# A token-sorted mixture of low-rank experts on one core: tiles of one expert instead of two, its projections made beforehand

## The reference

```python
conf = sigmoid(einsum('bsh,eh->bse', x, conf_W) + conf_b)
top_bids, sel = top_k(conf * expert_wealth, 2)
routing = softmax(top_bids)
for e in range(8):
    g = x @ base_gate + x @ gate_A[e] @ gate_B[e] * 0.25
    u = x @ base_up   + x @ up_A[e]   @ up_B[e]   * 0.25
    h = silu(g) * u
    oe = h @ base_down + h @ down_A[e] @ down_B[e] * 0.25
    out += sum(routing * (sel == e), -1)[..., None] * oe
return x + tanh(g_ffn) * out
```

## Time and profile before

| | |
|---|---|
| median of 3 runs | 350.17 us (349.76 to 350.34) |
| profiled execution: span from first to last instruction | 343.0 us |
| TensorE busy | 262.8 us, 77% |
| VectorE busy | 220.6 us, 64% |
| ScalarE busy | 160.7 us, 47% |
| GpSimd busy | 129.1 us, 38% |
| moved by DMA | 45.67 MB, 133 GB/s |

### The profile page before, as it was taken

How to read it: one execution, slowest core, us unless ns; L and a number is a source line. 1 busy time by engine, 2 the same in 40 slices (tenths; PEclk the granted TensorE clock), 3 DMA queues, 4 the chain that set the end, 5 groups by cost and what they waited for, 6 DMA issues and landing times.

```text
span 343.0 us, 5103 instructions
## 1 busy us (share of the span) xinstructions
PE 262.8 (77%) x1500; PEld 229.4 (67%) x1501; DVE 220.6 (64%) x433; ACT 160.7 (47%) x277; POOL 129.1 (38%) x148
## 2 busy tenths in 40 slices
PE   3474363537278899995999999999999999998600
PEld 2251241214167799994999999999999999997500
DVE  2979975798952881006666777777777777775325
ACT  0443875196336363343455555555555555555211
POOL 3528376537441441109233333333333333311121
PEclk9996566555579899998999999999999999999965
DMA  7803333013663646446244444434344444420065
GB/s 259 240 23 80 70 84 84 26 51 107 177 158 134 210 167 267 175 164 214 44 139 139 139 138 133 143 135 141 134 138 142 138 136 138 140 106 15 15 193 190
DMA packets 30189, 45.67 MB, mean 133 GB/s; under 512 B 13976, under 2 KB 25632, under 8 KB 30176
## 3 DMA queue, kind: packets, MB, share of 16 engines
q0 software_dynamic: 4416, 21.50, 18.9%
q1 hardware_dynamic: 20752, 14.03, 14.6%
q10 hardware_dynamic: 5008, 9.98, 7.9%
HBM read 33.57 MB, written 11.93 MB: 133 GB/s over the span
## 4 chain that ended last, share of the span: by engine, by line
PE 65%; DVE 17%; issue 5%; DMA 4%; POOL 3%; ACT 3%; SPq 1%; DVEq 0%; ACTq 0%; POOLq 0%
PE pY L55 8%; PE pY L59 7%; PE pY L57 7%; PE pG L55 5%; PE pT L1395 5%; PE pG L59 4%; PE pG L57 4%; PE pU L57 4%; PE pU L55 4%; PE pU L59 4%; DMA x_resid<-in_x_dram 2%; DVE q L899 2%; DMA yr<-results 1%; DVE q L819 1%; DVE am L821 1%
## 5 line engine op out<-in xcount | busy, mean ns | idle before, releaser
L496 POOL DMA_INDIRECT results<-yb,dest x19 | 19.0, 998 | 91.9 <-DVE yb L1108 91.9
L55 PE MATMUL pY<-Wd_hi,hT_hi 128*128 128x384 f32 x133 | 47.5, 357 | 0.9 <-ACT Wd_lo L694 0.8
L59 PE MATMUL pY<-Wd_hi,hT_lo 128*128 128x384 f32 x133 | 44.7, 336 | 0.0
L57 PE MATMUL pY<-Wd_lo,hT_hi 128*128 128x384 f32 x133 | 44.6, 336 | 0.0
L490 POOL DMA_INDIRECT bin<-base_products,tok x18 | 22.0, 1221 | 24.8 <-PE pU L59 15.2
L704 ACT CAST hT_hi<-pT 128x896 fp32r<-128x896 f32 x19 | 17.2, 907 | 24.1 <-PE pT L1395 24.1
L680 ACT CAST xaT_hi<-pX 128x256 fp32r<-128x256 f32 x19 | 7.1, 373 | 42.5 <-PE pX L1372 42.0
L55 PEld LDWEIGHTS pY<-Wd_hi,hT_hi 128*128 128x128 f32 x133 | 25.0, 188 | 2.3 <-DVE hT_lo L1096 1.0
L57 PEld LDWEIGHTS pY<-Wd_lo,hT_hi 128*128 128x128 f32 x133 | 25.1, 188 | 0.0
L482 POOL DMA_INDIRECT xin<-normed,tok x19 | 18.6, 979 | 16.9 <-PE pX L1358 9.9
L59 PEld LDWEIGHTS pY<-Wd_hi,hT_lo 128*128 128x128 f32 x133 | 25.0, 188 | 0.0
(11 more groups left out here) (260 smaller groups left out, 742.2 us busy)
## 6 DMA issues: line engine op xcount, KB each, us to landing
base_products<-brow ACTq DMA_DIRECT2D x8, 896.0 KB, 3.9
yr<-results SPq DMA_DIRECT2D x8, 256.0 KB, 4.6
raw<-in_L_ffn_gate_B_dram SPq DMA_DIRECT2D x8, 224.0 KB, 2.7
raw<-in_L_ffn_up_B_dram SPq DMA_DIRECT2D x8, 224.0 KB, 2.5
raw<-in_L_ffn_down_A_dram SPq DMA_DIRECT2D x7, 256.0 KB, 3.0
x_resid<-in_x_dram SPq DMA_DIRECT2D x4, 256.0 KB, 4.8
q<-in_fside_BxS2xS_dram ACTq DMA_DIRECT2D x4, 256.0 KB, 5.7
normed<-q ACTq DMA_DIRECT2D x4, 256.0 KB, 2.8
```

Source lines behind the costliest of these rows:

```text
L55: m.matmul(outs[i], hi, whi[i], start=first, stop=False, skip_group_check=True)
L57: m.matmul(outs[i], hi, wlo[i], start=False, stop=False, skip_group_check=True)
L59: ins = m.matmul(outs[i], lo, whi[i], start=False, stop=last, skip_group_check=True)
L496: g.indirect_dma_start(out=yg, out_offset=bass.IndirectOffsetOnAxis(ap=dest[:, j:j + 1], axis=0), in_=yb[:, :], in_offset=None).then_inc(d ...
```

## The change

- `GE` becomes 1: a tile has one expert, there are G = 8 groups, and PT = 23. The masks go, `z_copy` takes their place for z and writes z twice, side by side.
- `WA` is no longer applied in the loop. Before the loop TensorE makes for each of the 8 blocks of tokens the gate and up projections of all 8 experts (`products`, kind 2: 12 matmuls of 512 columns), ScalarE scales and copies them and writes them to the new tensor `projected`. Base gate, base up and projections are now 24 items, each with a copy and a write of its own, over 3 buffers. `normed` is not written any more.
- GpSimd's `gather` fetches 128 values a row from `projected`, gate and up side by side. Two buffers. `gather_base` now serves tile 0 too.
- `xa_T` is one transpose; gate is on rows 0 to 63 and up on rows 64 to 127. `WB` holds gate_B and up_B of an expert on the same two halves, and `expand` makes gate and up as matmuls of 64 rows in turn, 12 of 448 columns in all.
- The tile's `WB` is first copied to a fixed place: `WBe_hi` by ScalarE (`stage_B`), `WBe_lo` by GpSimd (`stage_B_lo`, 896 columns).
- The down products are 320 columns wide. `pY` has two banks; z and xa share one bank and one copy (`xz_hi_copy`). The high and low parts of z are the two halves of one operand, so that `WdB` needs 2 matmuls; `down_B` is loaded to both halves.
- h is transposed, split and used in two parts (4 and 3). The order of `tile` on each engine is new.

```diff
-GE = 2
+GE = 1
@@ weights
-            for gu, w in enumerate((gate_A, up_A)):
-                add([(view(len(chunks)).rearrange("p (e r) -> p e r", e=E), w[:, c * P:(c + 1) * P, :].rearrange("e h r -> h e r"))],
+            for e in range(0, E, 4):
+                to = view(len(chunks)).rearrange("p (e a r) -> p e a r", e=4, a=2)
...
+                add([(to[0:R, 0:IH], gate_B[e][:, cols]), (to[R:P, 0:IH], up_B[e][:, cols])], WB_hi[:, e, cols], WB_lo[:, e, cols], IH)
@@ GpSimd
             lo(CH_1 - lo_done[0])
+            pool.wait_ge(s_made, 2 * NT)
+            lo(CH_2 - CH_1)
             def gather(j):
-                if j:
-                    pool.wait_ge(s_xT, j)
-                g.indirect_dma_start(out=xin[:, :], out_offset=None, in_=xn,
+                if j >= 2:
+                    pool.wait_ge(s_xzT, j - 1)
+                g.indirect_dma_start(out=xin[:, j % 2, :], out_offset=None, in_=xa_rows,
...
+            pool.wait_ge(s_made, ITEMS)
+            for i in range(3):
+                pool.wait_ge(d_bn[i], 16 * ITEMS // 3)
+            def stage_B_lo(j):
+                e = pool.value_load(gid[0:1, j:j + 1], min_val=0, max_val=E - 1)
+                if j:
+                    pool.wait_ge(s_exp, j)
+                g.tensor_copy(WBe_lo[:, :], WB_lo[:, bass.ds(e, 1), :].rearrange("p a i -> p (a i)")).then_inc(s_WBl, 1)
+            for j in range(2):
+                gather(j)
+                gather_base(j)
+            stage_B_lo(0)
+            lo(NCH - CH_2)
+            stage_B_lo(1)
+            for j in range(2, PT + 3):
+                if j < PT:
                     gather(j)
                     gather_base(j)
+                    stage_B_lo(j)
                 if j >= 3:
                     scatter(j - 3)
@@ ScalarE
+            def tile(j, first=False, ahead=2):
+                h_hi(j, 0, first)
+                h_hi(j, 1, first)
+                e = expert(j + 2) if ahead == 2 else None
+                if ahead == 2:
+                    stage_B(j + 2, e)
+                if ahead >= 1:
+                    silu(j + 1)
+                xz_hi_copy(j, not first, ahead == 2)
+                if ahead >= 1:
+                    e = expert(j + 1)
+                    stage_dA(j + 1, 0, e)
+                    stage_dA(j + 1, 1, e)
@@ VectorE
+                if not first:
+                    z_copy(j - 1, 1 - par, second)
+                h_lo(j, 0)
+                h_lo(j, 1)
+                if ahead >= 1:
+                    g_add(j + 1, 1 - par)
+                    u_add(j + 1, 1 - par)
+                if not first:
+                    z_lo(j - 1)
+                if ahead == 2:
+                    xa_lo(j + 2)
+                if ahead >= 1:
+                    h_mul(j + 1)
+                if not first:
+                    y_copy(j - 1, 1 - par, second)
@@ TensorE
+            for t in range(NT):
+                products(2 * NT + t)
+            pe.wait_ge(s_copied, ITEMS)
...
+            def expand(j):
+                pe.wait_ge(s_xalo, j + 1)
+                pe.wait_ge(s_WBe, j + 1)
+                pe.wait_ge(s_WBl, j + 1)
...
+                    for k, (x_, w_) in enumerate(((xaT_hi, WBe_hi), (xaT_hi, WBe_lo), (xaT_lo, WBe_hi))):
+                        m.matmul(pG[:, i, 0:IH], x_[0:R, :], w_[0:R, cols], start=(k == 0), stop=(k == 2))
+                        ins = m.matmul(pU[:, i, 0:IH], x_[R:P, :], w_[R:P, cols], start=(k == 0), stop=(k == 2))
+                ins.then_inc(s_exp, 1)
...
+            def tile(j, par, first=False, ahead=2):
+                h_T(j, ahead == 0)
+                if ahead >= 1:
+                    expand(j + 1)
+                down_products(j, par, range(0, 4))
+                pe.wait_ge(s_hlo, 2 * j + 2)
+                if not first:
+                    ins = z_T(j - 1)
+                if ahead == 2:
+                    ins = xa_T(j + 2, par)
+                ins.then_inc(s_xzT, 1)
+                down_products(j, par, range(4, IC))
+                if not first:
+                    down_B_products(j - 1, 1 - par, expert(j - 1))
```

More of the change, by code:

```diff
@@ L352, in build @@
                 Wd_hi[:, c0:c1, 0:H], Wd_lo[:, c0:c1, 0:H], w)
+        CH_2 = len(chunks)
+        for e in range(0, E, 2):
+            to = view(len(chunks)).rearrange("p (e h) -> p e h", e=2)
+            src = down_B[e:e + 2].rearrange("e r h -> r e h")
+            add([(to[0:R], src), (to[R:P], src)], WdB_hi[:, e:e + 2, :], WdB_lo[:, e:e + 2, :], 2 * H)
         NCH = len(chunks)
@@ L738, in _ @@
+            e = expert(0)
+            stage_B(0, e)
+            xz_hi_copy(-2, z=False)
+            stage_dA(0, 0, e)
+            stage_dA(0, 1, e)
+            split(NCH - CH_2, NCH)
+            e = expert(1)
+            stage_B(1, e)
             silu(0)
-            xa_hi(1)
-            tile(1, back2=False)
-            tile(2, back3=False)
-            with act.Fori(3, PT - 1) as j:
+            xz_hi_copy(-1, z=False)
+            tile(0, first=True)
+            tile(1)
+            with act.Fori(2, PT - 2) as j:
@@ L743, in _ @@
                 tile(j)
[L744 to L750 removed]
+            tile(PT - 2, ahead=1)
+            tile(PT - 1, ahead=0)
+            xz_hi_copy(PT, xa=False)
             for b in range(0, NB, 2):
@@ L1107, in y_copy @@
                     dve.wait_ge(d_y, 16 * j)
-                v.tensor_copy(yb[:, :], pY[:, 0:H]).then_inc(s_yc, 1)
-            def tile(j, slot, back2=True, back3=True, last=False):
-                if back2:
-                    z_lo(j - 2)
-                h_lo(j - 1)
-                if back2:
-                    y_copy(j - 2, not back3)
-                g_add(j, slot)
-                if not last:
-                    x_lo(j + 1)
-                u_add(j, slot)
-                h_mul(j)
-                if not last:
-                    xa_mask(j + 1)
-                    xa_lo(j + 1)
-                z_mask(j - 1, not back2)
@@ L1127, in _, with tile @@
-            x_lo(0)
-            xa_mask(0, True)
-            xa_lo(0)
-            x_lo(1)
-            for i in range(2):
-                dve.wait_ge(d_bn[i], 16 * NT // 2)
-            g_add(0, 0, True)
-            xa_mask(1)
-            u_add(0, 0, True)
+                v.tensor_copy(yb[:, :], pY[par][:, 0:H]).then_inc(s_yc, 1)
+            def tile(j, par, first=False, second=False, ahead=2):
+                if not first:
[13 more added lines that the diff above has]
+                    y_copy(j - 1, 1 - par, second)
@@ L1136, in _ @@
+            xa_lo(0)
+            g_add(0, 0)
+            u_add(0, 0)
             xa_lo(1)
             h_mul(0)
-            tile(1, 1, back2=False)
-            tile(2, 0, back3=False)
-            tile(3, 1)
-            with dve.Fori(4, PT - 2, 2) as j:
+            tile(0, 0, first=True)
+            tile(1, 1, second=True)
+            with dve.Fori(2, PT - 3, 2) as j:
                 tile(j, 0)
                 tile(j + 1, 1)
-            tile(PT - 1, (PT - 1) % 2, last=True)
-            z_lo(PT - 2)
@@ L1146, in _ @@
-            h_lo(PT - 1)
-            y_copy(PT - 2)
-            z_mask(PT - 1)
+            tile(PT - 3, 0)
+            tile(PT - 2, 1, ahead=1)
+            tile(PT - 1, 0, ahead=0)
+            z_copy(PT - 1, 0)
             z_lo(PT - 1)
-            y_copy(PT - 1)
+            y_copy(PT - 1, 0)
             for b in range(NB):
@@ new lines, in h_T @@
+            def h_T(j, last=False):
+                pe.wait_ge(s_h, j + 1)
+                if not (isinstance(j, int) and j == 0):
+                    pe.wait_ge(s_hlo, 2 * j)
+                for half, chunks_ in enumerate((range(0, 4), range(4, IC))):
+                    if half and not last:
+                        pe.wait_ge(s_xalo, j + 2)
+                    if half and not (isinstance(j, int) and j < 2):
+                        pe.wait_ge(s_zlo, j - 1)
+                    for c in chunks_:
+                        ins = m.transpose(pT[:, half, (c % 4) * P:(c % 4 + 1) * P], hbuf[:, c * P:(c + 1) * P], ident[:, :])
+                    ins.then_inc(s_hT, 1)
@@ L1481 @@
+            xa_T(0, 0).then_inc(s_xzT, 1)
+            expand(0)
+            xa_T(1, 1).then_inc(s_xzT, 1)
+            tile(0, 0, first=True)
+            tile(1, 1)
+            with pe.Fori(2, PT - 3, 2) as j:
+                tile(j, 0)
+                tile(j + 1, 1)
+            tile(PT - 3, 0)
+            tile(PT - 2, 1, ahead=1)
+            tile(PT - 1, 0, ahead=0)
+            z_T(PT - 1).then_inc(s_xzT, 1)
+            down_B_products(PT - 1, 0, expert(PT - 1))
 _INS = ['x', 'fside_BxS2xS2_0', 'ctx_1024', 'g_xattn', 'g_ffn', 'L0_ffn_expert_wealth', 'L0_ffn_conf_W', 'L0_ffn_conf_b',
```

506 lines of the change are left out of this document (188 added, 318 removed).

## The result

| | before | after |
|---|---|---|
| median of 3 runs | 350.17 us (349.76 to 350.34) | 371.70 us (370.82 to 372.53) |
| ratio, 95% interval | | 1.0607 (1.0563 to 1.0651) |
| profiled execution, span | 343.0 us | 369.0 us |
| profiled execution, its time | not given | 370.8 us |
| TensorE, VectorE, ScalarE, GpSimd busy | 262.8, 220.6, 160.7, 129.1 us | 263.0, 222.5, 184.4, 161.8 us |

The change makes the kernel 21.5 us slower: 371.7 us, where 382.3 was forecast with a range of 362 to 398. The period of the loop was forecast at 7.24 us and is 7.13 from end to end of `h_mul` (7.15 from start to start), but the reason given for it, a collision of `h_mul` with GpSimd's copy, isn't in the trace.

The account below looks back on a forecast made before the run. TensorE was taken to bound the kernel, full in the loop at 8.51 us a tile. Forecast: 189.3 to the first `h_mul` end + 22 x 7.24 (159.3) + 26.5 tail = 375.1, plus 7.2 = 382.3 us; range 362 to 398.

Parts of the forecast that it names:

- TensorE's own work for a tile: Tile loop: TensorE's sum falls to 5.6 us a tile (6.7 with row halves one after the other), against 8.5.
- The pairs: Expansion: gate and up matmuls run side by side on the row halves, 6 pairs at 0.22, 1.35 us.
- The loop becomes a chain: Tile loop: steps across engines from one `h_mul` to the next give an undisturbed period of 6.5 us.
- GpSimd: Tile loop: its `WB_lo` copy, 1.25 us, lies across the start of `h_mul` and holds it; period 7.24 us.
- rival 2: Tile loop: GpSimd's copy misses `h_mul`, period 6.5 us, 365 us in all; chance 0.2.
- Landing of `gather_base`: Tile loop: rows land at 9.03, wanted by `g_add` at 9.69; hidden with 0.7 us to spare.
- Before the loop: Stretch to the first `h_mul` end: new projections of 22.7 us lie on the path; 189.3 us, 28.0 later.
- Tail: After the last `h_mul`: shorter down products and earlier, narrower `WdA` staging; 26.5 us instead of 28.5.
- What lies around the span: Outside the profiled span: 7.2 us, the median of 350.17 above the span, added at the end.
- halves one after the other: Expansion: row halves do not overlap, `expand` ends at 3.5, period 7.55 us, 391 us in all; chance 0.2.
- the copy at the two-input rate: Tile loop: GpSimd's copy ends at 7.16, period 8.25 us, 405 us in all; chance 0.07.
- TensorE as the bound: Tile loop: VectorE's chain does not hold, TensorE sets a period of 5.6 us, 345 us; chance 0.04.

Follow-up runs that it names:

- e3b: Changed kernel with the six up matmuls of each expansion waiting until the six gate matmuls have landed; 404.18 us.
- e3_halves_apart: Changed kernel with the expansion issued in another order, for each half of the columns three gate matmuls, then three up matmuls; 371.15 us.
- e9: Changed kernel with only `xa_lo` moved behind `h_mul`, and the gather of tile j+1 put behind GpSimd's copy of tile j; 364.43 us.
- e2: Changed kernel with a second GpSimd copy, 1792 columns into an unused buffer, behind each copy of `WB_lo`; 384.81 us.
- e5: Changed kernel with `h_mul` put ahead of `z_lo` and `xa_lo` on VectorE; 375.37 us.
- e6: As e5, with the `WdB` product moved between the halves of the next tile's h transposes and `z_copy` ahead of `y_copy`; 384.52 us.

## Why the prediction was right, and where it wasn't

**TensorE's own work for a tile: right.** 5.6 us were forecast. In the tile above it goes from the first transpose at 255.69 to the last product of `WdB`, which starts at 261.74, 6.05 us, and with 0.12 for that product (an estimate from the start of the one before it) 6.2. Of that 0.3 is the wait for `hT_lo` and 0.25 the gap ahead of the transposition of `xin`. The pairs came as taken: 0.20 apart against 0.22, and e3b shows that the second half costs nothing. The Trainium skill, "TensorE: Matmul & The Clock Gate", Part 3: Packing small matmuls, has the overlap right; it also says that matmuls never change their order, while in e3_halves_apart an up matmul issued three behind its gate matmul starts 0.01 us after it.

**The loop becomes a chain: right, its undisturbed length mis-sized.** 6.46 us were forecast, 7.12 to 7.15 measured, with no disturbance by the copy. By steps, counted from the start of one `h_mul` to the next in the tile above: the transposes start at 1.22 where 1.14 was taken, and the expansion at 2.13 where 1.94 was. From the start of its last pair (3.26) to `g_add` (4.00) are 0.74 us where the forecast had 0.47. So `g_add` is 0.46 late by this point, the largest term: 0.08 ahead of the transposes, 0.11 as they take 0.91 from first start to the expansion and not 0.80, and 0.27 behind the last pair. From `g_add` to `silu` and its end the forecast holds (1.12 against 1.12); `xz_hi` starts 0.1 behind `silu`'s end, and from `z_lo` to `h_mul` it is 0.54 instead of 0.42. So 0.35 of the 0.66 are two hand-overs from one engine to the next that take longer than I had put them; 0.23 are steps of one engine that follow each other less closely; and the 0.1 ahead of `xz_hi` is the late `xin`, as e9 shows, in which it is gone.

**GpSimd: wrong.** This is the step of the prediction that failed: the overlap of the copy with `h_mul`. The forecast had the copy from 4.9 to 6.15 after the end of `h_mul`, across the next `h_mul` at 5.37, with a period of 7.24. Two terms failed. The copy takes 0.94 instead of 1.25, below the lower bound of 1.1 that I had worked out from the two-input subtraction, and the gaps ahead of `gather_base` and of the copy are 0.30 and nothing instead of 0.53 each. (`gather_base` itself was taken at 0.94, where its row has 1.25; it does take 0.94 here.) So it ends at 5.10 by that count (260.65 against 255.55), and `h_mul`, by the longer chain, comes at 6.04. The copy misses it: rival 2, for which I had 0.2, with its price wrong too, as the 365 us rested on the short chain. Two errors cancelled: 0.66 us a tile that the chain is longer, and 0.78 for a collision that isn't there. So that the period came out within 0.1 us is luck, and by its own sign, `h_mul` keeping its 1.09, this part of the prediction is wrong. The mechanism itself is real: e2, e5 and e6 show `h_mul` at 1.66, 1.69 and 2.10 beside a copy. The Trainium skill, "SBUF — State Buffer", SBUF: two separate sides, says that the first to start keeps the port pair for its whole instruction. In e2 and e5, where the copy starts first, the trace agrees: `h_mul` ends 0.95 to 0.96 us behind the copy's end. In e6 the trace differs: `h_mul` starts 0.06 to 0.40 us ahead of the copy, and still the copy keeps its 0.94 and `h_mul` ends 0.95 to 0.96 behind it. GpSimd issues `gather_base` up to the start of the copy there; whether that is the reason wasn't tested.

**Landing of `gather_base`: right, that of `gather`: left out.** No wait for `bin` is in the loop. But the forecast followed only this transfer; the one of `xin`, issued at 1.93 and needed by its transposition, was never set against its need, and TensorE waits for it in the loop (2.9 us in 11 of 18 tiles). That ring, together with the `h_mul` held beside the copy, undid e5 and e6.

**Before the loop: 28.0 forecast, 22.0 measured.** Projections 22.4 against 22.7. From their end (143.47 + 22.4) to the first gather 4.8 against 5.1. Gathers and first copy 5.9 against 7.0, the short copy and gaps again. The expansion at half clock, to `g_add`, 2.65 against 2.7. To the end of `h_mul` 4.0 against 4.2. These terms differ by 2.1 together; 0.5 of them is a slip in adding (170.1 + 1.0 + 3.5 is 174.6, not 174.9, and 182.2 + 2.7 is 184.9, not 185.1). The other 3.9 are ahead of the projections: base tile 4 starts at 123.67 instead of 127.64, and 2.6 of that is there already at the first base tile (95.62 against 98.22). In the traces of the experiments, which change nothing up to there, that tile starts between 95.86 and 97.93, so about 2 of it moves from run to run; the rest wasn't followed up.

**Tail: 26.5 forecast, 29.0 measured.** From the end of the last `h_mul` to that of the last copy to `yb` were 11.2 us before and are 9.5 now, 1.7 less where 2.0 was forecast. `yb` has one buffer, and this last copy has to wait for the scatter of the tile before it:

```profile
349.13 0.42 DVE L1093 COPY yb<-pY 128x256 f32<-128x256 f32 x1 [1.55 <-DMA results<-yb,dest]
```

From there to the end, which I had taken to stay as it was, 17.3 us became 19.5 (18.9 to 19.7 in the traces of the experiments). 0.7 of it is there by the last step of VectorE, as the results read back land later (median 5.4 us instead of 4.6), and 1.4 comes behind that step. Why they land later, and what the 1.4 are, stays open.

**What lies around the span: 7.2 forecast, 1.8 measured.** This term was made by setting the median of one set of executions against the span of another. Without it the sum is 375.1, and a span of 369.0 came. Against the 370.8 us of the profiled execution the forecast of 382.3 is 11.5 too high: 6.0 before the loop, 2.5 in it, 5.4 around the span, less 2.5 for the tail. It also means that the 26.0 between the two spans is not the 21.5 between the medians.

The rivals: the copy that misses `h_mul` is what happened, at 371.7 and not the 365 put beside it; halves one after the other (391) is excluded by e3b; the copy at the two-input rate (405) by the 0.94; TensorE as the bound (345) by its idle time ahead of the transposes.

## What to carry to other kernels

When a change frees the engine that was the bound, the loop falls back on its longest ring, and each hand-over in it counts: here the chain was 0.66 us of 7.12 longer than the sum, 0.35 of it in hand-overs. A period that comes out right can hide this, so look for the mechanism's own sign in the trace, here the length of `h_mul`. Draw every ring, that of the gathers through the issuing queue too, before shortening one: e5 and e6 shortened the first, ran into the second and moved `h_mul` onto the copy. And work that is moved out of a loop to the front of it has to be paid at once, while the loop gives its gain back only as far as the next ring lets it.
